# Where the value tiles of an attention unit stand among the score matmuls of their step

## The reference, cut to what matters

```python
q = _heads(hidden_states @ to_q_w)
h_txt = _sdpa(q, _heads(ehs_txt @ to_k_w), _heads(ehs_txt @ to_v_w))
h_obj = _sdpa(q, _heads(ehs_obj @ to_k_object_w), _heads(ehs_obj @ to_v_object_w))
h_oth = _sdpa(q, _heads(ehs_oth @ to_k_others_w), _heads(ehs_oth @ to_v_others_w))
h_ip = _sdpa(q, _heads(ehs_ip @ to_k_ip_w), _heads(ehs_ip @ to_v_ip_w))
out = _merge(h_txt) + SCALE_OBJ * _merge(h_obj) + SCALE_OTH * _merge(h_oth) + SCALE_IP * _merge(h_ip)
out = out @ to_out_w + to_out_b
out = (out + residual) / RESCALE
```

## Time and profile before

| | before |
|---|---|
| median of 3 runs | 2498.65 us (2498.43 to 2501.18) |
| profiled execution: span from the first to the last instruction | 2497.3 us |
| PE busy | 2464.5 us (99%) |
| ACT busy | 1705.2 us (68%) |
| DVE busy | 1596.6 us (64%) |
| POOL busy | 411.6 us (16%) |

### The profile page before, as it was taken

How to read it: one execution, slowest core, us unless ns; L and a number is a source line. 1 busy time by engine, 2 the same in 40 slices (tenths; PEclk the granted TensorE clock), 3 DMA queues, 4 the chain that set the end, 5 groups by cost and what they waited for, 6 DMA issues and landing times.

```text
span 2497.3 us, 37368 instructions
## 1 busy us (share of the span) xinstructions
PE 2464.5 (99%) x13125; PEld 1830.2 (73%) x13125; DVE 1596.6 (64%) x2961; ACT 1705.2 (68%) x3830; POOL 411.6 (16%) x567
## 2 busy tenths in 40 slices
PE   8999999999999999999999999999999999999998
PEld 7999999999999995466666666656666666666655
DVE  4131111111211248899999999999999999999993
ACT  3132212211212238999999999999999999999994
POOL 0000000000000013333133122222231231221310
PEclk9999999999999999999999999999999999999999
DMA  9473323323324257667677677667676666676761
GB/s 242 130 246 131 121 87 123 132 103 122 111 93 175 108 108 171 106 148 154 124 146 150 132 145 146 130 151 143 127 151 137 140 144 132 149 147 123 152 137 49
DMA packets 287618, 341.25 MB, mean 137 GB/s; under 512 B 89406, under 2 KB 181694, under 8 KB 287430
## 3 DMA queue, kind: packets, MB, share of 16 engines
q1 hardware_dynamic: 234032, 275.93, 49.7%
q10 hardware_dynamic: 53398, 62.93, 7.8%
HBM read 186.71 MB, written 83.89 MB: 108 GB/s over the span
## 4 chain that ended last, share of the span: by engine, by line
PE 93%; ACT 4%; issue 1%; DVE 1%; ACTq 1%; DMA 0%; SPq 0%
PE s_ps L1311 17%; PE st_ps L1284 16%; PE s_ps L429 13%; PE om_ps L463 12%; PE st_ps L449 12%; PE om_ps L481 11%; PE om_ps L504 10%; ACT s_ps L600 2%; ACT probs L592 1%; PE om_ps L1331 1%; ACTq L1099 1%; PE st_ps L1311 1%; PE s_ps L518 0%; PE st_ps L1260 0%; PE om_ps L1260 0%
## 5 line engine op out<-in xcount | busy, mean ns | idle before, releaser
L600 ACT ACTIVATE s_ps<-s_ps,negmax 128x427 f32<-128x427 f32 x1280 | 762.7, 602 | 25.3 <-DVE small L664 25.2
L655 DVE TENSOR_REDUCE negmax<-s_ps 128x2 f32<-128x854 f32 x640 | 667.1, 1042 | 79.5 <-PE s_ps L429 79.0
L592 ACT ACTIVATE probs<-st_ps 128x1024 f32<-128x1024 f32 x632 | 655.0, 1036 | 36.3 <-PE st_ps L449 31.3
L429 PE MATMUL s_ps<-kpack,qpack 96*128 96x512 f32 x1280 | 429.9, 417 | 7.2 <-ACT s_ps L600 4.3
L1311 PE MATMUL s_ps<-w_split,ctx_split 128*128 128x320 f32 (+2 forms) x2928 | 432.1, 309 | 1.9 <-DVE w_split L1192 1.9
L1284 PE MATMUL st_ps<-ctx_split,w_split 128*128 128x428 f32 (+2 forms) x2280 | 428.2, 348 | 4.6 <-DVE ctx_split L1192 4.6
L1311 PEld LDWEIGHTS s_ps<-w_split,ctx_split 128*128 128x128 f32 (+2 forms) x2928 | 429.9, 186 | 2.9 <-DVE w_split L1192 2.2
L1284 PEld LDWEIGHTS st_ps<-ctx_split,w_split 128*128 128x128 f32 x2280 | 409.8, 189 | 19.7 <-DVE ctx_split L1192 4.9
L449 PE MATMUL st_ps<-qpack,kpack 104*128 104x512 f32 x1264 | 408.9, 405 | 8.1 <-ACT probs L592 6.7
L429 PEld LDWEIGHTS s_ps<-kpack,qpack 96*128 96x128 f32 x1280 | 212.8, 189 | 252.8 <-ACT s_ps L600 220.8
L397 POOL TENSOR_TENSOR small<-small,negmax 128x616 f32<-128x616 f32 x160 | 196.1, 1226 | 1150.3 <-DVE negmax L672 1150.3
(11 more groups left out here) (76 smaller groups left out, 1526.4 us busy)
## 6 DMA issues: line engine op xcount, KB each, us to landing
kpack<-kT SPq DMA_DIRECT2D x240, 256.0 KB, 5.1
qpack<-q_out SPq DMA_DIRECT2D x240, 256.0 KB, 5.8
kT<-k_out ACTq DMA_DIRECT2D x160, 217.5 KB, 2.2
ctx_split_raw<-in_ctxT SPq DMA_DIRECT2D x128, 214.0 KB, 4.2
xs_raw<-in_xT SPq DMA_DIRECT2D x85, 256.0 KB, 4.7
out<-in_xT SPq DMA_DIRECT2D x75, 256.0 KB, 6.0
out_yT<-out SPq DMA_DIRECT2D x75, 256.0 KB, 3.4
v_ip_rows<-v_out ACTq DMA_DIRECT2D x48, 320.0 KB
```

What stands on the lines that cost most here:

```text
L429: last = nc.tensor.matmul(s_ps[:, n % 2, z, :], qpack[r][0:ROWS_S, j, t * P:(t + 1) * P], kpack[r][0:ROWS_S, j, :], start=True, stop=True)
L592: nc.scalar.activation(probs[:, at:at + 2, :], transposed(u, duo), ACT.Exp).then_inc(p_done, 1)
L600: last = nc.scalar.activation(s_ps[:, n % 2, z, SMALL:TOK], s_ps[:, n % 2, z, SMALL:TOK], ACT.Exp, bias=negmax[:, r, IP, j, t:t + 1], accu ...
L655: nc.vector.tensor_reduce(negmax[:, r, IP, j, t0:t0 + 2], s_ps[:, n % 2, :, SMALL:TOK], AX_X, ALU.max, negate=True).then_inc(s_max, 1)
```

## The change

The three value tiles of steps 0, 2 and 4 stood directly behind the transposed scores of their step, ahead of the score pair. Now they stand behind the score pair, ahead of the products that follow it. The fourth, of step 6, stood behind the score pair already (step 6 has no products behind it) and stays in its place. No instruction is added or removed, on any engine, and the lists of ACT, DVE, POOL and SP are the same as before.

```diff
                 if unit(u):
                     scores_t(u, duo)
-                if k in (0, 2, 4) and unit(m - 4):
-                    values(m - 4, k // 2)
                 products_at(m, k, Q_AHEAD_FIRST if alone else Q_AHEAD, Y_AHEAD)
                 u, p = pair_at(m, k + 1) if k + 1 < STEPS else pair_at(m + 1, 0)
                 if unit(u):
                     scores(u, p)
+                if k % 2 == 0 and unit(m - 4):
+                    values(m - 4, k // 2)
                 products_at(m, k, Q_BEHIND_FIRST if alone else Q_BEHIND, Y_BEHIND)
-                if k == 6 and unit(m - 4):
-                    values(m - 4, k // 2)
```

## The result

| | before | after |
|---|---|---|
| median of 4 runs | 2498.54 us (2497.76 to 2501.18) | 2591.10 us (2587.97 to 2594.28) |
| ratio after / before | | 1.0367, 95% interval 1.0352 to 1.0381 |
| profiled span | 2497.3 us | 2592.4 us |

The change makes the kernel 3.7% slower. The forecast was 2583, with a range of 2545 to 2610.

A forecast was written before the change was run, and what follows sets the result against it. PE was taken to set the pace, with ACT only 2.5% behind. 83 us from 71 slots and 2 us from the others made the span 2582.3, given as 2583 us after rounding; range 2545 to 2610.

The forecast's parts named there:

- No gain is to be had: PE in mid-attention: a stream without idle time (500.00 of 500 us busy) can only get longer by another order.
- The tile's own waits: nothing: Value tiles on PE: their waits for probabilities, and ACT's wait for the tile, were to cost nothing more.
- Step 0: a stall of 0.59 and 0.10 for weights: Score pair of step 0: waits 0.59 us for ACT's exponentials of step 7, then 0.10 for weights not loaded ahead.
- Step 2: no stall, since step 0 has paid: Score pair of step 2: PE already 0.71 us late, so ACT's exponentials of step 1 are done; no stall.
- Step 4: 0.37 by way of ACT's `probs` of step 2: Score pair of step 4: ACT, delayed by late transposed scores in step 2, makes PE stall 0.37 us, plus 0.10 for weights.
- Rivals 1 and 2: Stalls in a slot: only that of step 0 remains, 2548 us, chance 0.12; or all three stall, 2628 us, chance 0.08.
- 71 x 1.17 = 83: Slots 9 to 79, which hold both projections: each loses about 1.17 us, 83 us in all.
- 2 us for the rest: Slots 4 to 8 without output products and 80 and 81 without query products: 0.3 us each, 2 us in all.
- The clock stays at 1.00: PE's granted clock in the changed kernel's profile: was to stay at 1.00, under which the forecast would be wrong.
- rival 3: PE's clock drops behind the stalls: 1.7 us more in each of 71 slots, 121 us, about 2704 us; chance 0.05.
- Rivals 4 and 5: Whole kernel: the move does nothing, 2498.65 us, chance 0.04; or tiles avoid their 0.08 and 0.10, 2460 us, chance 0.02.

The follow-up runs named there:

- the shorter exponentials: ACT's exponentials of the 427 remaining keys leave out the last 140 columns: 2491.27 us in the order of before, 2545.45 us in the changed order.
- the kernel with products as cover: Changed kernel with the four query products of step 4 ahead of its score pair, except in early slots: 2569.83 us, ratio 1.0279 to the kernel before.

## Why the prediction was right

- **No gain is to be had.** Right for all the orders tried: 500.00 of 500 us busy before, and each of them lost.
- **The tile's own waits: nothing.** Right for this change, but the list was short of one: the tile of step 0 also waits until DVE has copied the heads of the unit before. Moved behind its pair it comes later and doesn't feel it; with all four tiles in front this wait is what it stands in.
- **Step 0: a stall of 0.59 and 0.10 for weights.** Measured 0.59; the transposed scores of step 1 take 0.56 to the products, as forecast. Alone it costs 0.72 a slot. That it hangs on ACT is shown by the shorter exponentials.
- **Step 2: no stall, since step 0 has paid.** Right (0.46), and shown by the kernels with step 2 alone (0.57) and with steps 0 and 2 (nothing more).
- **Step 4: 0.37 by way of ACT's `probs` of step 2.** Measured 0.36, with the forecast wait of ACT ahead of it (0.48 in the row). Rivals 1 and 2, one stall or three, are out.
- **71 x 1.17 = 83.** Measured 71 x 1.211 = 86.0. Averaged over these slots the two stalls are 0.60 and 0.38, which is half of the 0.04 by which the slot lost more; the rest is in no one place.
- **2 us for the rest.** This term was mis-sized: 95.1 - 86.0 = 9.1. In the profiled execution the early slots lost 0.5 each and not 0.3, four of them 2.0; the one with the low clock 4.7, of which 4.2 through the clock; 2.3 lie behind the last marker. This and the 0.04 explain why the time was 8 us above the forecast.
- **The clock stays at 1.00.** Right in the slots with output products, wrong in one early slot and in the last ones, where the window 2542 to 2548 has 0.50. In the early slot rival 3 happened in small, 4 us instead of 121: there the two waits of 0.8 were 1.5 us apart, as in the earlier trace rows, and not 10 us like the stalls of this change. That the trace of before has a drop only behind the two late waits was a misreading: its window 33 to 37 has 0.57 as well, in the first part, where PE had been idle for 4.6 us. The Trainium skill, "TensorE: Matmul & The Clock Gate", section on psum-queue depth-cycling, says of one kernel that short idles of PE between groups of matmuls, frequent enough, made the clock swing between its two rates. The traces here don't bear it out as a forecast: two stalls in each slot of the main stretch did not lower the clock, and of two kernels with the same pair of idles in the early slots one kept the full clock.
- **Rivals 4 and 5** are out by the result: the kernel is 3.7% slower.

## What to carry to other kernels

On an engine that is busy all the time, an instruction's place is worth what it covers: before one is moved, list the waits that stand behind it and read for each how long the releaser's last row ends after the time at which the waiting one could start. Walk the whole cycle with the delays carried along, since a stall pays for later waits only as far as the other engine isn't waiting for this one in between. And an instruction that covers one wait makes what stands behind it later for another engine: here the tile has to be in front of the pair in steps 0, 2 and 4 (for ACT) and behind it in step 6 (for DVE).

## What the hardware showed that was not expected

In the changed kernel two waits of PE of 0.81 and 0.79 us, 1.5 us apart, were followed by some 10 us at a granted clock of 0.50, in which a value tile took 1.94 instead of 1.06 us. In the kernel with products as cover the same two waits in the same slot, 0.82 and 0.79 us, were followed by the full clock. So these waits alone don't decide it; what else does stays open.
